# A graph-network kernel on one core: ten rounds a turn in the loop of the dense counts, eight steps a turn in the typed attention's sums

## What is computed

```python
msg = h[s] * norm[:, None]
out = jax.ops.segment_sum(msg, d, num_segments=num_nodes)
```

```python
denom = jax.ops.segment_sum(ex, col_idx, num_segments=n)
alpha = ex / denom[col_idx]
agg = jax.ops.segment_sum(alpha[..., None] * msg_edge, col_idx, num_segments=n)
```

## Time and profile before

| | |
|---|---|
| median of 3 runs | 6112.72 us (6111.27 to 6112.85) |
| profiled execution, its own time | 6110.95 us |
| its span, first to last instruction | 6109.3 us |
| mean granted clock of TensorE | 0.837 |
| dense counts, within the span | about 528 to 912 us |
| typed attention's sums, within the span | about 3160 to 3405 us |

### The profile page before, as it was taken

One profiled execution on the slowest core, in us unless ns is written; L12 is line 12 of the kernel. 1 busy time (PEld: TensorE's weight loads), 2 busy tenths in 40 slices (PEclk: granted clock), 3 DMA queues, 4 the chain that ended last, 5 costly groups with the idle time before them and its releaser, 6 DMA issues. The chain is left out here.

```text
span 6109.3 us, 86221 instructions
## 1 busy us (share of the span) xinstructions
PE 4559.6 (75%) x23040; PEld 3253.8 (53%) x23041; DVE 3431.3 (56%) x7298; ACT 1669.5 (27%) x3845; POOL 2360.8 (39%) x2718
## 2 busy tenths in 40 slices
PE   5876878845549969566669889999999395465568
PEld 1213435634337745354446677768888363355546
DVE  8987883556682345699948634441112333655544
ACT  0864653411102235111100333333222121200022
POOL 0742005547608833677500058401111301477700
PEclk8998999955559989788769989999999597667779
DMA  0002437512120048999847110004333331233300
GB/s 31 2 11 92 165 159 239 181 31 35 26 72 19 8 131 330 320 329 323 255 159 236 59 31 12 11 31 133 102 103 102 97 103 53 75 103 102 99 19 21
DMA packets 392653, 673.68 MB, mean 110 GB/s; under 512 B 115915, under 2 KB 280915, under 8 KB 387819
## 3 DMA queue, kind: packets, MB, share of 16 engines
q1 hardware_dynamic: 295938, 420.30, 21.6%
q0 software_dynamic: 96320, 250.79, 13.2%
q10 hardware_dynamic: 192, 0.15, 0.0%
HBM read 440.60 MB, written 229.81 MB: 110 GB/s over the span
## 5 line engine op out<-in xcount | busy, mean ns | idle before, releaser
L1106 PE MATMUL wsum_a_ps<-wsum_a_hot,wsum_a_rows 128*128 128x128 f32 x1664 | 323.1, 373 | 235.6 <-DMA wsum_a_rows<-table,edge_src 126.9
L1092 POOL DMA_INDIRECT wsum_a_rows<-table,edge_src x416 | 414.6, 997 | 214.2 <-issue 118.5
L2192 POOL DMA_INDIRECT big<-hgt_table,edge_key x416 | 393.6, 946 | 174.3 <-issue 131.3
L1106 PEld LDWEIGHTS wsum_a_ps<-wsum_a_hot,wsum_a_rows 128*128 128x128 f32 x1664 | 296.5, 276 | 262.2 <-DVE big L1133 177.9
L3446 PE MATMUL sagel_ps<-sagel_piece,sagel_high 128*128 128x448 f32 x1050 | 398.4, 379 | 0.8 <-issue 0.8
L3446 PE MATMUL sagel_ps<-sagel_piece,sagel_low 128*128 128x448 f32 x1050 | 384.7, 366 | 0.0
L3390 POOL CAST sagel_piece<-x 128x1792 fp32r<-128x1792 f16 (+1 forms) x75 | 112.8, 1504 | 682.0 <-PE sagel_ps L3446 411.8
L787 PE MATMUL cnt_ps<-cnt_hot_s,cnt_hot_d 128*128 128x512 bf16 x1760 | 318.3, 334 | 66.6 <-DVE cnt_hot_s L769 64.1
L2240 PE MATMUL hgt_s_pq<-big 128*128 x1248 | 227.1, 345 | 169.1 <-DVE hgt_s_tmp L2279 135.3
L2192 POOL DMA_INDIRECT big<-gat_table,own_src x288 | 272.4, 946 | 90.5 <-issue 86.6
L1902 ACT ACTIVATE soft_h<-soft_ps,soft_b,soft_v 128x320 f32<-128x320 f32 x320 | 197.6, 618 | 336.7 <-PE soft_ps L1868 336.7
(11 more groups left out here) (984 smaller groups left out, 11199.0 us busy)
## 6 DMA issues: line engine op xcount, KB each, us to landing
hgt_edge_values<-big SPq DMA_DIRECT2D x104, 512.0 KB
big<-hgt_edge_values SPq DMA_DIRECT2D x104, 512.0 KB, 4.4
x<-counts SPq DMA_DIRECT2D x75, 448.0 KB, 3.3
x<-counts SPq DMA_DIRECT2D x75, 336.0 KB, 2.9
counts<-big SPq DMA_DIRECT2D x25, 832.0 KB, 3.4
counts<-big SPq DMA_DIRECT2D x25, 768.0 KB, 3.2
big<-counts SPq DMA_DIRECT2D x30, 640.0 KB
counts_turned<-big SPq DMA_DIRECT2D x30, 640.0 KB
```

The lines of the kernel that those rows point to most:

```text
L1092: nc.gpsimd.indirect_dma_start(rows[n % DEEP][:, u, :], None, table, bass.IndirectOffsetOnAxis(ap=e.src[:, g:g + 1], axis=0)).then_inc(gat ...
L1106: mm = nc.tensor.matmul(ps[r.slot % 2][u][:, k * P:(k + 1) * P], rows[r.slot][:, u, k * P:(k + 1) * P], hot[r.slot % 2][:, u, :], start=Tr ...
L2192: nc.gpsimd.indirect_dma_start(rows[n % DEEP][:, u, :], None, at.table, bass.IndirectOffsetOnAxis(ap=at.index[:, g:g + 1], axis=0)).then_i ...
```

## The change

The body of the loop of the dense counts holds ten rounds where it held two, on VectorE and on TensorE: 11 turns for 55. The body of the loop of the attention's sums holds eight steps where it held four: 13 turns for 26. Buffers, their number and the order of all operations are as before; in the sums, the value that VectorE waits for is worked out from the turn and from which half of the body a step is in. No other function differs.

```diff
--- before.py
+++ after.py
@@ -707,8 +707,9 @@
 
     groups, visits = e.groups, e.visits
     COLUMNS = groups + 1
-    RING, OUT = 4, 3
+    RING, OUT, BODY = 4, 3, 10
     BASE = RING + 1
+    assert visits % (RING * BODY) == 0
     REGION = 2048
     WIDE = NP - FIRST_HALF
     WIDTH = HALVES[1][1]
@@ -751,15 +752,15 @@
                     link(nc.vector.memset(source[:, half * COLUMNS + groups:(half + 1) * COLUMNS], 0.0))
                     link(nc.vector.memset(target[:, half * COLUMNS + groups:(half + 1) * COLUMNS], 999.0))
 
-                with dve.Fori(0, visits // RING // 2) as j:
-                    for h in range(2):
-                        first = (j * 2 + h) * RING
+                with dve.Fori(0, visits // RING // BODY) as j:
+                    for h in range(BODY):
+                        first = (j * BODY + h) * RING
                         buckets = numbers(nc, mybir.EngineType.DVE, e.visit_bucket[0:1, ds(first, RING)], 2 * NT - 1)
                         places = numbers(nc, mybir.EngineType.DVE, column[0:1, ds(first, RING)], 2 * COLUMNS - 1)
 
                         dve.wait_ge(done, first + BASE - RING)
                         for u in range(RING):
-                            nc.vector.tensor_scalar(hot_d[h][:, u, :], iota16[:, 0:P], target[:, ds(places[u], 1)], None,
+                            nc.vector.tensor_scalar(hot_d[h % 2][:, u, :], iota16[:, 0:P], target[:, ds(places[u], 1)], None,
                                                     ALU.is_equal).then_inc(ends_made, 1)
                         for u in range(RING):
 
@@ -775,16 +776,16 @@
                 pe.wait_ge(step, SETUP)
 
                 pe.sem_inc(done, BASE)
-                with pe.Fori(0, visits // RING // 2) as j:
-                    for h in range(2):
-                        first = (j * 2 + h) * RING
+                with pe.Fori(0, visits // RING // BODY) as j:
+                    for h in range(BODY):
+                        first = (j * BODY + h) * RING
                         regions = numbers(nc, mybir.EngineType.PE, region[0:1, ds(first, RING)], REGION)
                         pe.wait_ge(ends_made, first + RING)
                         for u in range(RING):
                             pe.wait_ge(matched, first + u + 1)
                             for lo in range(0, WIDTH, 512):
                                 n = min(512, WIDTH - lo)
-                                mm = nc.tensor.matmul(ps[:, ds(regions[u] + lo, n)], hot_d[h][:, u, :],
+                                mm = nc.tensor.matmul(ps[:, ds(regions[u] + lo, n)], hot_d[h % 2][:, u, :],
                                                       hot_s[u][:, lo:lo + n], start=False, stop=False,
                                                       skip_group_check=True)
                             mm.then_inc(done, 1)
@@ -2567,6 +2568,8 @@
     W = H + HV
     groups = e.groups
     steps = groups // R
+    BODY = 2 * DEEP
+    assert steps % BODY == 0
     BASE = R + 1
     REGION = 512
     with ExitStack() as c:
@@ -2595,9 +2598,9 @@
                 link(nc.vector.tensor_scalar(region[:], region[:], float(REGION), None, ALU.mult))
                 link(nc.vector.memset(zeros[:], 0.0))
                 nc.vector.memset(ps[:], 0.0).then_inc(moved, 2)
-                with dve.Fori(0, steps // DEEP) as j:
-                    for k in range(DEEP):
-                        n = j * DEEP + k
+                with dve.Fori(0, steps // BODY) as j:
+                    for k in range(BODY):
+                        n = j * BODY + k
 
                         dve.wait_ge(done, n * R + BASE - R)
                         nc.vector.tensor_tensor(hot[k % 2][:], kit.iota[:, None, :].broadcast_to([P, R, P]),
@@ -2605,9 +2608,9 @@
                                                 ).then_inc(matched, 1)
                         weight = weights[:, ds(n * R, R), :]
                         nc.vector.tensor_copy(val[k % 2][:, :, 0:H], weight).then_inc(weighed, 1)
-                        dve.wait_ge(loaded[k], j * 16 + 16)
+                        dve.wait_ge(loaded[k % DEEP], (j * (BODY // DEEP) + k // DEEP) * 16 + 16)
                         nc.vector.tensor_tensor(val[k % 2][:, :, H:].rearrange("p r (h d) -> p r h d", h=H),
-                                                rows[k].rearrange("p r (h d) -> p r h d", h=H),
+                                                rows[k % DEEP].rearrange("p r (h d) -> p r h d", h=H),
                                                 weight[:, :, :, None].broadcast_to([P, R, H, dv]), ALU.mult
                                                 ).then_inc(valued, 1)
 
@@ -2616,9 +2619,9 @@
                 pe.wait_ge(ready, 3)
 
                 pe.sem_inc(done, BASE)
-                with pe.Fori(0, steps // DEEP) as j:
-                    for k in range(DEEP):
-                        n = j * DEEP + k
+                with pe.Fori(0, steps // BODY) as j:
+                    for k in range(BODY):
+                        n = j * BODY + k
                         blocks = numbers(nc, mybir.EngineType.PE, e.blk[0:1, ds(n * R, R)], NT - 1)
                         regions = numbers(nc, mybir.EngineType.PE, region[0:1, ds(n * R, R)], REGION)
                         pe.wait_ge(matched, n + 1)
```

## The result

The changed kernel takes 6131.43 us (median of nine runs, 6121.75 to 6137.05) against 6111.66 us for the kernel before in the same session (nine runs, 6104.48 to 6118.11): ratio 1.0032, 95% interval 1.0021 to 1.0042. It is **slower by 0.3%**, some 20 us. 6122 us was predicted, within 6086 to 6148; the likeliest case, VectorE fetching its loop again, is the one that came, at a higher price. By the prediction's own mark of 12 us this counts as slower, to which it had given 0.27, less than to either other outcome.

The account below looks back on a forecast made before the run. In the counts TensorE and VectorE, both nearly full, wait for each other at round edges, neither alone the limit. 17.6 + 0.7 us gained, 28 lost: 9.7 more than 6110.95, plus 1.8 to the median, 6122 us, range 6086 to 6148.

Parts of the forecast that it names:

- The edges: Dense counts: 44 of 54 edges between turns vanish at 0.4 us each, 17.6 us gained, ends 0 and 39.6.
- The cap of 66.6 us: Dense counts: TensorE's idle time, the most that any edit to the loop's control could give back.
- The sums: Attention's sums: 13 of 25 edges vanish at 0.05 us each, 0.7 us gained, ends 0 and 5.2.
- The cap taken from TensorE's 28.2 us of idle time: Attention's sums: TensorE is idle 28.2 us in the whole stage, said to cap the gain there.
- The refetch: Counts' back edge on VectorE: loop head fetched again ten times at 2.8 us, 28 us lost, 10.6 to 44.
- Rival 3: Counts' back edge: more than one fetch stops VectorE each turn, another 28 us, 6150 us; chance 0.13.
- case 1: The forecast: VectorE fetches its counts loop's head again once a turn, 6122 us, 6105 to 6139; chance 0.45.
- case 3: Same as Rival 3: more than one fetch stops VectorE in each turn of the counts, 6150 us; chance 0.13.
- Rival 2: Counts: VectorE holds the whole turn, only the edges count, 6094 us, from 6070 to 6106; chance 0.37.
- TensorE charged nothing: Counts: TensorE's turn grows from 110 to 550 instructions, judged to fit what it holds, so no loss charged.
- case 2: Same as Rival 2: VectorE holds the whole turn of the counts, 6094 us, from 6070 to 6106; chance 0.37.
- The Trainium skill's rule: VectorE's counts loop: 32 KB of instructions, stall on branching to code not held; spoke against ten rounds a turn.

Follow-up runs that it names:

- c3: Kernel before with only the sums' loop at eight steps a turn, counts at two rounds, wait values bounded: sums 232.5 us, whole kernel 1.0010 of before.
- e4: Kernel before with all 110 rounds of the counts (both engines) and the 104 steps of the sums written out: counts 343.6, sums 223.7 us, kernel 0.9929 of before.
- c2: The change with the sums back at four steps, only the counts at ten rounds a turn: counts 399.5 us, whole kernel 1.0034 of before.
- d2: Counts at ten rounds, sums at four steps, plus one instruction on VectorE hinting the back edge at each turn's head: counts 362.8 us, kernel 0.9975 of before.
- e1: Counts at ten rounds, sums at four steps, VectorE's loop head placed at the 96th instruction of a piece: counts 414.7 us, kernel 1.0069 of before.
- d1: Counts at ten rounds, sums at four steps, VectorE's loop head placed at the start of a piece of 128: counts 363.0 us, kernel 0.9975 of before.
- d4: Kernel before with ten rounds a turn on TensorE alone, VectorE at two, sums at four steps: counts 375.6 us, kernel 0.9997 of before.
- c4: Kernel before with all 110 rounds of the counts written out on VectorE and TensorE, sums at four steps: counts 342.2 us, kernel 0.9943 of before.

## Why the prediction was right, and where it was off

- **The edges: 44 x 0.4 = 17.6 us gained.** Right. Without refetches the counts take 363.0 us against 381.4 and 380.1 with two rounds a turn (both bounded): 17.1 to 18.4, which is 0.39 to 0.42 us an edge. Reading the edge from the sequencer's starts was better than the idle times, whose upper end was twice that. It was luck in one respect: the single engines' runs show that 0.4 is a sum of two parts that partly hide each other, not TensorE's edge alone.
- **The cap of 66.6 us** was read too high: of that idle time of TensorE, 15.45 us lie before the first matmul of the stage, ahead of any back edge, which leaves 51. The line is from the kernel before:

```profile
533.09 3.27 PE L787 MATMUL cnt_ps<-cnt_hot_s,cnt_hot_d 128*128 128x512 bf16 x9 [15.45 <-DVE cnt_hot_s L769]
```

- **The sums: 0.7 us gained.** Not to be told from nothing. 231.1 became 230.5 in the change, but c3 has 232.5, and the kernels with four steps spread from 231.1 to 232.6. The cap taken from TensorE's 28.2 us of idle time was no cap: e4 gained its 7.9 us with the idle times as they were, since the ends of the matmuls are modelled.
- **The refetch.** Right in mechanism and place: once for each of ten back edges, with 57 packets in the counts (more than 20 was the mark), 2.8 to 5.0 us from the branch of line 755 to the head where 0.3 is usual, and TensorE idle behind it. VectorE's turn is the 292 instructions counted, over four pieces of 8.1 KB. All five pieces came anew in each turn, not the head alone; behind the second, no interval between rounds is over 0.3 us longer in c2 than in d2.
- **The step that was mis-sized is its price**: 2.8 us was taken from the shortest transfer from HBM shown, and it measured (399.5 - 362.8)/10 = 3.7 us. That is 37 us lost for 28, and it explains the miss: 37 - 18 = 19 us, and 20 was measured, for 9.7 forecast. Two things were left out. The missing head costs 3.2 us in the mean (the interval between rounds across the turn is 6.90 us in c2 and 3.71 in d2), so the price lay between the two rows named, 2.8 and 4.4 us. And the second piece is not wholly covered: the next interval but one, where it begins to be needed, is 3.86 us in the mean of ten turns for 3.34.
- **Rival 3** had this second piece as a whole second stall, 56 us. It decided, by its own line, from 3.05 us a turn, and the turn lost 3.7. So what came lies between case 1 and case 3; the argument that fetching ahead should cover a second piece held but for 0.5 us of it. In e1, where that interval is 4.69 us, it held less.
- **Rival 2, VectorE holds the turn: 6094 us.** d1 is that case made true by placement, with the sums at four steps: 6093.9 us. The prediction noted that the edge between two pieces may lie within the loop of today, and left the pieces that 292 instructions touch at three or four. From 30 instructions ahead of an edge it is four, from a piece's start, three. The trace of the kernel before has the place: a small packet comes when the engine enters a piece, and the one of the first turn came some 30 instructions behind the loop's head. How many pieces are held, no row of it shows, so the case could not be decided from the rows alone.
- **TensorE charged nothing.** Right: two large packets in the counts, both in the first turn, the second 1.1 us ahead of its first back edge, and none at the nine behind it; and d4 shows ten rounds on it as a gain.
- **Slips in the sums.** The upper end of case 1 is 6138 us for the 6139 given, the lower end of case 2 6068 for 6070; nothing hangs on either.
- **The Trainium skill's rule**, "Runtime: NRT & Kernel Launch", section "Instruction fetch mechanics": a taken branch to a block no longer held stalls. The trace agrees, at 3.7 us. By the two lines of 16 KB of "Advanced Engine Details and Errata", section "Sequencer and Instruction Queues", an estimate is that d1 and e1 both touch at least two lines and fetch one ahead, three for two held, so that both would stall; d1 doesn't, and four pieces of 128 fit all the runs.

## What to carry to other kernels

Before a loop body is made longer, count its instructions on each engine and find where the head lies in the pieces of code (a small instruction packet marks each piece entered): here the turn and the one piece ahead must fit in four pieces of 128, and beyond that every back edge costs 3.7 to 5.2 us against 0.4 us that an edge is worth. A loop's edge and its register work can be on the path though both engines look busy: with 110 rounds and 104 steps, writing them out beat every loop here, since code in a row was fetched without a pause over 0.3 us (c4). Measure both engines' loops together; either alone showed nothing here.

## What was not expected of the hardware

- The same 292 instructions took 363.0 or 414.7 us of stage by the slot of their first one, and the kernel 6093.9 or 6152.6. An edit that adds instructions ahead of such a loop would move it too, so an unrelated change may cost or gain almost 1% of this kernel; that was not run.
- The hint for the branch (39 ns once a turn) helped in another way than its name says: no packet for the head came at all in d2, but the piece behind the loop was not fetched any more, and a turn over four pieces then fits.
- Entering a loop through the padding costs once: in d1 the first branch to the head takes 2.8 us until the head's first operation, the ten others 0.3.
- A branch back into a piece just thrown out took from 2.8 to 5.0 us to its target in c2 and the change, 3.3 to 5.3 in e1, though such a packet itself takes 0.3 to 1.0 us. The spread goes with the stores of the counts. Of the 30 pauses of c2, the change and e1, the nine over 4.5 us have 224 to 288 packets of stores starting in them, the 21 under 4 us have 0 to 180. A longer pause also has room for more packets, and no run was made without the stores, so this cause is likely and not shown. The packets of the stores and of the code within two pauses of the changed kernel, one of 4.75 us (638.3 to 643.0, two rows) and one of 2.79 (675.3 to 678.0, its only row):

```profile
q1 hardware_dynamic: 288, 1.18, 62.9%
q14 instruction: 2, 0.02, 0.8%
...
q14 instruction: 1, 0.01, 0.7%
```
